# The one-hots turned for the sort's start table: two operations of the Scalar engine in place of one of VectorE

## What is computed

```python
edge_index = jnp.stack([src, dst])
h = jnp.maximum(_layernorm(x, axis=-1), 0.0)
x = x + _L0_gnn_ref(h, edge_index, edge_attr_3, ...)   # three spline convolutions
h = jnp.maximum(_layernorm(x, axis=-1), 0.0)
x = x + _L1_gnn_ref(h, edge_weight1, edge_index, ...)  # two scatter-adds and four dense tanh layers
```

## Time and profile before

| | us |
|---|---|
| median of 3 runs | 15,764.69 (15,753.51 to 15,776.48) |
| the profiled execution | 15,624.22 |
| its span | 15,622.4 |
| sort's second pass, POOL's first to last slot write | 2,382.6 |

### The profile page before, as it was taken

The page is one execution under the profiler, slowest core; times in us unless marked ns, Lnnn a source line. Parts: engine busy times, 40 slices in busy tenths (PEclk is TensorE's granted clock), DMA queues, the critical chain, the costliest instruction groups (busy, mean ns, idle before and its releaser), DMA issues. The chain is left out here.

```text
span 15622.4 us, 398079 instructions
## 1 busy us (share of the span) xinstructions
PE 10863.1 (70%) x143261; PEld 9126.5 (58%) x143262; DVE 7757.7 (50%) x17968; ACT 5731.3 (37%) x11114; POOL 7310.4 (47%) x7201
## 2 busy tenths in 40 slices
PE   7566656553666666666666666777777776899998
PEld 7556556442555555555555554555555555888887
DVE  6567667684222222222222223444444445888887
ACT  0000000242343444444444342433333334666665
POOL 0577777786444444444444433344343442433333
PEclk6555555565666666666666676777777777767777
DMA  1122222101111111111110001111111112344443
GB/s 44 48 65 70 67 59 69 44 2 21 25 25 24 25 24 25 24 25 24 25 24 9 7 7 31 34 35 34 34 35 34 35 34 67 129 128 128 129 128 104
DMA packets 787752, 741.20 MB, mean 47 GB/s; under 512 B 319931, under 2 KB 570623, under 8 KB 786911
## 3 DMA queue, kind: packets, MB, share of 16 engines
q1 hardware_dynamic: 604284, 655.86, 13.7%
q0 software_dynamic: 183392, 84.32, 3.3%
HBM read 529.76 MB, written 63.39 MB: 38 GB/s over the span
## 5 line engine op out<-in xcount | busy, mean ns | idle before, releaser
L1318 POOL DMA_INDIRECT c_near<-h_rows,c_idx x2368 | 2371.3, 1001 | 3128.5 <-DVE c_near_apart L1371 2379.0
L1404 ACT ACTIVATE c_products<-c_pa 125x512 f32<-125x512 f32 x2368 | 2189.1, 1077 | 3302.8 <-remote 1647.2
L1448 PE MATMUL c_pa<-c_near_apart,c_basis 32*125 32x128 f32 x18944 | 1673.1, 355 | 1736.3 <-ACT c_products L1404 874.6
L1448 PEld LDWEIGHTS c_pa<-c_near_apart,c_basis 32*125 32x125 f32 x18944 | 1251.5, 237 | 2167.2 <-issue 2163.1
L1361 DVE TENSOR_TENSOR c_basis<-c_outer,c_hats 128x1000 f32<-128x1000 f32 x296 | 355.3, 1200 | 3934.6 <-PE c_pa L1448 2341.4
L1724 POOL DMA_INDIRECT edges_b<-c_send_rows,c_send_idx x1184 | 1251.5, 1057 | 2044.9 <-DMA c_send_idx<-edge_idx 1728.8
L746 POOL DMA_INDIRECT slots<-slot_stage,slot_idx x1568 | 1826.9, 1165 | 575.5 <-issue 555.1
L1882 ACT ACTIVATE c_products<-c_pa 125x256 f32<-125x256 f32 x2368 | 1162.2, 647 | 2118.2 <-DMA dst_rows<-rows_dst 1146.2
L1458 PE MATMUL c_py<-c_products,c_weights 125*64 125x128 f32 x18944 | 1672.2, 338 | 136.8 <-issue 135.8
L1458 PEld LDWEIGHTS c_py<-c_products,c_weights 125*64 125x64 f32 x18944 | 1446.5, 176 | 267.5 <-issue 208.1
L2370 PE MATMUL acc_mi_mo<-msg,hot_e 128*128 128x32 bf16 x11328 | 1386.4, 192 | 80.4 <-DVE hot_e L2249 65.5
(11 more groups left out here) (370 smaller groups left out, 21465.5 us busy)
## 6 DMA issues: line engine op xcount, KB each, us to landing
own_d<-hparts SPq DMA_DIRECT2D x1888, 96.0 KB, 1.9
rows<-local_rows SPq DMA_DIRECT2D x472, 256.0 KB, 3.5
hi_rows_in<-hi_rows SPq DMA_DIRECT2D x392, 256.0 KB
c_dst_rows_in<-dst_rows SPq DMA_DIRECT2D x148, 512.0 KB
rows_both<-hi_rows SPq DMA_DIRECT2D x196, 196.0 KB
c_near<-h_rows,c_idx POOLq DMA_INDIRECT x2368
near_h<-c_near_h SPq DMA_DIRECT2D x148, 256.0 KB
c_near<-near_h SPq DMA_DIRECT2D x148, 256.0 KB, 2.7
```

What stands on the lines that cost most here:

```text
L1318: pool.indirect_dma_start(near[:, half, q, :], None, g.h1_rows, bass.IndirectOffsetOnAxis(idx[:, half, q:q + 1], 0), bounds_check=last_nod ...
L1404: last = act.activation(by_round[:, half, r, rnd * TR:(rnd + 1) * TR], pa[0:K3, r, 0:TR * P].rearrange("p (j s f) -> p j s f", s=2, f=widt ...
L1448: last = pe.matmul(pa[0:K3, r, j * P:(j + 1) * P], basis[at, q // HALF, q % HALF, :], apart[at, q // HALF, q % HALF, :, :], start=True, st ...
```

## The change

The per-partition number `row_number` gets a negative twin `minus_row_number`, made once. DVE's compare L650 is taken out. ACT computes the same tile in two operations: Square of (row value minus row number), then Relu of (1 minus that), which is 1 where the two are equal and 0 elsewhere, as both are whole numbers. On ACT's queue this `turn(k+1)` stands behind the stage copy of step k and ahead of the start table of step k+1, and `turn(0)` at the head. It waits for the fill and for PE as the compare did; the Relu waits for the Square by a new semaphore `s_square`. SP waits for `s_square` too before it fills a half again.

```diff
--- before.py
+++ after.py
@@ -257,6 +257,7 @@
     row_of = sb("row_of_edge", [P, ET, SLOT_W])
     num = sb("num_row", [P, max(HI, 64), STEP], F16)
     of_s, of_b, row_b, row_no = (sb(n, [P, 1]) for n in ("rows_of_s", "rows_of_b", "row_in_b", "row_number"))
+    minus_row = sb("minus_row_number", [P, 1])
     pick_b, shift_b = sb("pick_b", [P, NA]), sb("shift_b", [NA, P])
     hot_row, hot_col = sb("hot_row", [P, 2, ROWS, STEP], F16), sb("hot_col", [P, 2, COLS, STEP], F16)
     NTR = -(-ET // P)
@@ -378,6 +379,7 @@
             st.add(dve.tensor_scalar(row_b[:, :], g.nodecol[:, 0:1], -float(HI), None, ALU.add))
             st.wait()
             st.do(dve.scalar_tensor_tensor(row_no[:, :], of_b[:, :], -float(HI), g.nodecol[:, 0:1], ALU.mult, ALU.add))
+            st.add(dve.tensor_scalar(minus_row[:, :], row_no[:, :], -1.0, None, ALU.mult))
             st.add(dve.tensor_scalar(pick_b[:, :], g.iotaf[:, 0:NA], row_b[:, :], None, ALU.is_equal))
             st.add(dve.tensor_scalar(shift_b[:, :], g.iotaf[0:NA, 0:P], float(HI), g.nodecol[0:NA, 0:1],
                                      ALU.subtract, ALU.is_equal))
@@ -598,7 +600,7 @@
     place_i, low_i, high_i = (sb(n, [P, 2 * STEP], I32) for n in ("place_si", "low_si", "high_si"))
     stage, idx = sb("slot_stage", [P, DEEP, STEP, SLOT_W]), sb("slot_idx", [P, DEEP, STEP], U32)
     s_row, s_row_free = [sem(f"s_hi_rows{h}") for h in range(2)], sem("s_hi_rows_free")
-    s_turned = sem("s_hots_turned")
+    s_turned, s_square = sem("s_hots_turned"), sem("s_hots_squared")
     s_hots, s_table, s_cnt, s_gat = (sem(n) for n in ("s_hots_s", "s_start_table", "s_counted", "s_places"))
     s_chosen, s_idx, s_idx_b = sem("s_chosen"), sem("s_slot_idx"), sem("s_bucket_idx")
     s_stage, s_sent = sem("s_slot_stage"), [sem(f"s_slots_sent{r}") for r in range(DEEP)]
@@ -619,6 +621,7 @@
                 for half in range(2):
                     k = i * 2 + half
                     sp.wait_ge(s_row_free, k + 1)
+                    sp.wait_ge(s_square, k + 1)
                     for kind in range(2):
                         sp.dma_start(rows[:, half, kind, :],
                                      g.hi_rows[kind:kind + 1, ds(k * STEP, STEP), :].rearrange("o t e -> o (t e)")
@@ -647,8 +650,6 @@
                 st = Steps(dve, s_hots, k * 3)
                 dve.wait_ge(s_row[half], filled * 64)
                 dve.wait_ge(s_gat, k + 1)
-                dve.tensor_scalar(turned[0:ROWS, half, :], rows_both[0:ROWS, half, :], row_no[0:ROWS, :], None,
-                                  ALU.is_equal).then_inc(s_turned, 1)
                 st.add(alike(same[:, half, :, :], rows[:, half, 0, :], hi16, k))
                 st.add(alike(same_b[:, half, :, :], rows[:, half, 1, :], sa16, k))
                 bucket_cells(dve, k, half)
@@ -694,6 +695,17 @@
 
         @block.scalar
         def _(act):
+            act.sem_inc(s_square, 2)
+
+            def turn(k, half, filled):
+                act.wait_ge(s_row[half], filled * 64)
+                act.wait_ge(s_gat, k + 1)
+                act.activation(turned[0:ROWS, half, :], rows_both[0:ROWS, half, :], ACT.Square,
+                               bias=minus_row[0:ROWS, :]).then_inc(s_square, 1)
+                act.wait_ge(s_square, k + 3)
+                act.activation(turned[0:ROWS, half, :], turned[0:ROWS, half, :], ACT.Relu, bias=g.onecol[0:ROWS, :],
+                               scale=-1.0).then_inc(s_turned, 1)
+
             def step(i, r, follows):
                 k, half = i * DEEP + r, r % 2
                 act.wait_ge(s_cnt, k + 1)
@@ -705,7 +717,10 @@
                 last.then_inc(s_table, 1)
                 act.wait_ge(s_sent[r], i * (STEP * 16) + 16)
                 act.activation(stage[:, r, :, :], row_of[:, ds(k * STEP, STEP), :], ACT.Copy).then_inc(s_stage, 1)
-
+                if follows:
+                    turn(i * DEEP + (r + 1), (r + 1) % 2, i * (DEEP // 2) + ((r + 1) // 2 + 1))
+
+            turn(0, 0, 1)
             all_steps(act, step)
 
         @block.tensor
```

## The result

| | before | after |
|---|---|---|
| median of 4 runs each, us | 15,759.1 (15,753.1 to 15,776.5) | 15,889.2 (15,861.2 to 15,900.0) |
| ratio after / before, 95% interval | | 1.0078 [1.0061, 1.0095] |
| the profiled execution, us | 15,624.2 | 15,900.0 |
| first to last slot write, us | 2,382.0 | 2,542.7 |
| mean slot write, us | 1.165 | 1.087 |

A forecast was written before the change was run, and what follows sets the result against it. POOL's slot writes in the sort's second pass were taken as the bound. Writes -18.1, start -1.3 and pauses +6 gave -13.4 us, taken off the median 15,764.7: 15,751 us, range 15,709 to 15,815.

The forecast's parts named there:

- The bound: Sort's second pass: POOL, 96% loaded, sets the end; only shorter POOL steps or fewer, shorter pauses help.
- The gain on POOL's writes: Slot writes in the sort's second pass get shorter without DVE's compare: -18.1 us, bounds 0 and -40.
- window of 67 writes: Slot writes starting 0.10 to 0.47 us ahead of `hot_turned`, together 18.1 us longer; taken as the whole gain.
- The 73 undisturbed writes: Slot writes overlapping `hot_turned` but no two-input operation, none over 0.98 us; read as evidence against a full lock.
- rival of a full lock: `hot_turned` shuts POOL out whenever they meet: 113 us gained, 15,652 us; chance 0.03.
- POOL's pauses: Long stops between slot writes: one in 14 steps instead of 16, nearly 2 more, up to +12, taken as +6 us.
- The slower rival: Landed writes to start table: 12 more pauses of 6.5 us, 15,823 us; chance 0.15, shared with an unlucky compare rhythm.
- ScalarE's pair, hidden: Square and Relu between stage copy and start table: 2.3 us a step, POOL's lead 34 to 32 us, price 0.
- SP's fills: SP's four transfers wait for the Square and go out some 7 us later in held steps; price 0.
- Start: Head of the pass: two `hot_turned` go from before the first slot index, -1.3 us.
- The free DVE step: DVE's step when not held falls from 9.0 to 8.4 us, hidden behind POOL's 12.2.
- The final sum: -13.4 us taken off the timed median 15,764.7, which lay 140.5 us above the profiled execution: 15,751 us.

The follow-up runs named there:

- A': Chip without long POOL pauses, on which the kernel before takes 11,759 us.
- e7: The kernel after, with DVE's compare put back into a tile nobody reads, on a chip with pauses: 15,766.3 us, 1.0001 against the kernel before.
- e5: The kernel after, unedited, run again on a chip with pauses: 15,860.7 us, 1.0062 against the kernel before.
- A: Another chip without long POOL pauses, on which the kernel before takes 11,755 us.
- e1: The kernel before, unedited, profiled a second time, on a chip without pauses: 11,761.8 us (one run).
- e8: The kernel after, unedited, on a chip without pauses: 11,673.3 us, 0.9926 against the kernel before.
- B: Chip with long POOL pauses, on which the kernel before takes 15,766 us.
- e13: The kernel before with 8 more one-column matmuls and their weight loads on PE each step, on a chip with pauses: 15,655.8 us, 1.0021.
- e6: The kernel after with ScalarE's pair moved ahead of the stage copy and its wait for landed writes, on a chip with pauses: 15,846.8 us, 1.0043.
- e14: The kernel after with each slot write cut to 64 of 128 partitions, on a chip with pauses: 15,780.8 us, 1.0101 against the kernel before.
- e9: The kernel after with a one-column POOL memset behind each slot write and a wait per step, chip without pauses: 11,826.8 us, 1.0056 against before.

## Why the prediction was wrong

**The bound.** Right: POOL's chain of writes set the end of the pass, and DVE's time was hidden. On A' the shorter writes came through to the microsecond. The statement that only a shorter POOL step or fewer and shorter pauses move the end was right too; both moved, in opposite directions.

**The gain on POOL's writes: -18.1 us, bounds 0 and -40.** This term was mis-sized. It measured -122 us between the two profiles, -128 us on one chip (e7 to e5: 1,176 to 1,094 ns) and -91 us on A and A' (e1 to e8). To find the missing part, all writes of a trace were sorted by when they start relative to DVE's next or last `same_hi` compare, and what each takes over 0.97 us was summed. The sums in us:

```
start against same_hi    before    e7      e5      e1      e8
-1.5 to  0 us              43.9    40.1     0.1    47.6     0.9
 0   to  2 us             158.9   158.1   124.7   135.8   116.5
 2   to  3 us              26.6    27.1    58.8    46.6    55.9
 3   to  5 us (masks)      75.2    95.9     8.6    55.1    20.6
```

The writes that start up to 1.5 us ahead of `same_hi`, those around `hot_turned` itself, lose their whole excess, 40 to 48 us: my window of 67 writes that start 0.10 to 0.47 us ahead of it was too narrow, as those which start inside it and run into `same_hi` were booked on the compare, though without `hot_turned` such writes are not longer. The larger part, by this table, is rhythm; no run tests it by itself. A stretched write ends with what stretched it, and so sets when the next ones start; without the first operation of the block the writes fall less on the masks (87 us less on B, 35 on A'), more on the stretch ahead of them (32 and 9 more); those of the first 2 us hold 33 and 19 us less. I had given rhythm a bound on the losing side only, +30 us. The 73 undisturbed writes of the earlier trace rows were true and proved less than I read from them: each of them started 0.47 us or more ahead of `hot_turned` and met it only with its last 0 to 0.5 us. A write that starts while `hot_turned` runs could not be among them, as it takes at least 0.97 us and `same_hi` begins 0.67 us behind the start of `hot_turned`; in before there are 126 such writes, and they hold 25.8 us of excess. The rival of a full lock, 196 x 0.58 = 113 us, came close in size.

The Trainium skill, "SBUF — State Buffer", section "Who interferes with whom", has a two-port `tensor_scalar` shut GpSimd out for the whole instruction. Whether this compare ran in that mode no row shows. The size agrees with it, 0.46 to 0.66 us per removed operation of 0.75; the place does so only in part, since a third to a half of that sits on writes that meet the operation.

**POOL's pauses: +6 us.** This is the step that failed and decided the sign. The prediction kept their number at one in 14 steps on the ground that nothing of PE's work changes. 12 became 60 (on one chip, 17 in e7 and 56 in e5), the idle before writes rose by 281.5 us, and the price of one was nearly right (5.8 us above the usual 0.30, against 6.5). The pauses hardly depend on how much PE does (15 in e13), but on how fast POOL's writes follow one another: e7 and e5 differ in nothing but DVE's compare, which makes that 1.484 instead of 1.410 us. The trace of before held the hint, in the first line of the table of late steps: 42 of 84 steps with little or middling stretch are late, and 1 of 96 with much. I had read that the crawls come "mostly when the steps have been held for a while"; that names many of the same moments and not the cause.

**The slower rival: more pauses, 15,823, chance 0.15.** Right in the place where the time is lost, wrong in mechanism and size. It put the cause into the chain of landed writes, stage copy, Square and start table (e6 excludes that) and priced 12 more pauses, where there are 39 more (e7 to e5) to 48 more (the two first profiles). It also set them against a gain of 19 us, not 122.

**ScalarE's pair, hidden.** Right: 2.3 us, start table 2.36 us behind the stage copy where 2.4 was said, lead 30.6 us in e8 where 32 was said (median 29.8, against 34.2 in e1), no price on A'. **SP's fills.** Right: in e8 SP issues at 1502.41, 1.4 us after the Square's start, and DVE's waits for fills are 66.9 us in all, at the start alone, as before (66.6). **Start.** -1.3 us did not come: the first write stands at 565.3, before at 565.4, since two ScalarE operations took the place of the one of VectorE. **The free DVE step.** Right: 8.28 us at its tenth percentile, 8.78 before. **Table load.** Right: the trace of after shows none in the pass, and the Square at 549.08 is followed by the Relu at 550.27 and the start table at 551.32.

**The final sum.** It took 140.5 us between profile and median as an unexplained offset. The offset was most likely another chip, and with it the number of pauses in the timed runs: 12 in the profile, an estimated 15 to 18 where the timing was done (12, and 3 to 6 more of 6.5 us for the 20 to 37 us by which the pass is longer there by the estimate above).

## What to carry to other kernels

When an engine that feeds a long chain gets faster, ask whether its pace itself is what the rest can bear: here a quicker GpSimd was a gain of 0.74% on a chip of one kind and a loss of 0.6 to 0.8% on those of the other. And when you put something in to slow an engine, measure the distances afterwards: the memsets vanished in gaps that were there anyway, and one wait a step did the work. A wait whose releaser is "remote", and single PE instructions with gaps of 0.5 to 2 us for no reason that the profile shows, are the mark of it; count them before and after, and see what the other engines did in the 10 to 20 us ahead. And compare an operation's effect on another engine by whole blocks and their rhythm, not by the writes that touch it.

## What the runs showed of the hardware

- The same program takes 11,755 or 11,759 us on two chips and 15,622 or 15,766 on two others. The idle time ahead of all instructions that write or read `c_pa` in the spline stages (PE's weight loads and matmuls, and ScalarE's copies), kernel before, first on the chip of the profile of before, then on A:

```profile
  issue: 3759.7, 4932
  remote: 1647.2, 202
  PE c_pa L1448: 1604.9, 379
```

```profile
  issue: 1492.3, 1200
  PE c_pa L1448: 1117.7, 588
```

  "Remote" is all ScalarE's, "issue" nearly all PE's: 2,714 us ahead of weight loads and 990 ahead of matmuls, on A 1,465 and 22. On A "remote" does not occur. So late signals and slow issue are not confined to the sort. These differences are of the size of the 3,900 us between the two kinds of chip, but the idle times of two engines overlap, and no run here tests what makes up the difference.
- A signal of PE reached two engines 6.5 us after the matmul that raised it, at the same moment, while PE ran on (after, 585.06 and 591.52).
- An indirect write of 64 slots takes 0.903 us of GpSimd in the median (e14), one of 128 slots 0.972 (after): 0.07 us for half the rows.
- A one-column memset on POOL takes 0.127 us. Behind an indirect write it lengthened the gap to the next write by 0.02 us in the mean (e9 against e8), as that gap of 0.305 us was there anyway. The wait for its semaphore, 0.89 us, lengthened the gap at the head of a step from 0.305 to 1.01 us.
